# Two picks a step instead of sixteen in one go: moving the scatters of the first attention's groups

## The chip, the cores and the metric

The kernel runs on one core of a Trainium2 chip. The metric is the device time of one execution in microseconds (us). The kernel before took 1837.02 us (median of three runs, 1831.98 to 1838.97).

## The reference

Two decoder layers on 16 sequences of 128 tokens and 256 channels. What the change touches lies in the first layer:

```python
x = x + attention(layernorm(x))           # 16 heads of 128
x = x + wkv(layernorm(x), ctx)            # per channel: a recurrence over the 128 tokens
h = layernorm(x)
probs = softmax(h @ router_w.T)           # 16 experts
top_vals, top_idx = top_k(probs, 4)       # four picks for every token
x = x + sum of the picked experts of h, weighted by top_vals, + a shared expert
```

Attention, a further cross attention and a ternary feed-forward of the second layer follow and are not touched.

## The kernel before, in words

The work is laid out by hand, engine by engine. There are four groups (g = 0 to 3) of four sequences. The first attention walks over 16 projections p (a group times a set of four heads), and each has four steps, one per sequence: NSTEP = 64 steps, n = 4p + b. The groups come one after the other: group 0 in steps 0 to 15, group 1 in 16 to 31, and so on.

In step n every engine does its part of three sequences at once: TensorE (PE) computes the scores of n (line 763), turns the probabilities of n - 2 (771), fills in three of the twelve parts of the next projection's queries, keys and values (595 to 597), multiplies the output of n - 3 (790) and the values of n - 2 (780). VectorE (DVE) takes a value part out of PSUM (1657), masks and reduces the scores (1663, 1666), normalises (1671, 1673) and adds the output to the residual (1680). ScalarE (ACT) takes the exponentials (2342) and copies the turned probabilities and the values out of PSUM (2350, 2355). PE may not start the output of the next sequence before DVE has added the last one (line 1680).

Beside these steps runs the next layer's work for the group whose attention is done. It is written as generators, and `side.step` advances each engine's own list by five moments per step. In step 20 (36, 52) the list of group 0 (1, 2) is added: `wkv_group` (39 moments, the recurrence in two halves of 128 channels), `routing` (25, the layer norm of the routed rows, the logits, the top four) and `dispatch` (9, where in the table of picked rows each pick goes). GpSimd (POOL) has three kinds of work there:

- `split_wqkv` (2702, 2704): it splits a third of the next projection's weights in two parts of lower precision. The load of a third is issued by SyncE (SP, `fetch_third`, 2925), which waits until the raw buffer is free, that is for an earlier split. In the third step of a projection (b = 2; 34, 38, 42 ...), once PE has done an output that SP waits for, SP issues the output weights and then zeros and weights in turn: six transfers of 512 KB.
- `wkv_helps` (2710, 2711): two products of the recurrence. They wait for ACT's exponentials, and DVE waits for them.
- `scatter(g, b)` (2723 to 2731): four indirect DMAs for sequence b of the group, one for each pick. Each writes 128 rows of 1 KB to the table `picked_inputs` in DRAM, at the rows that DVE put in `slots` (1478). They read the group's normalised rows in `tiles_xn`, one of two buffers.

The next user of that buffer is `normalised` of the next group's routing (1251 to 1262), on DVE: it waits until all sixteen scatters of the group have landed. The last reader of the table is the expert stage, after the attention.

## Time and profile before

| | us |
|---|---|
| median of three runs | 1837.02 |
| all three | 1831.98, 1838.97, 1837.02 |
| profiled execution: its own time | 1832.67 |
| its span in the trace | 1830.9 |
| PE busy | 1622.8 (89%) |
| DVE busy | 1132.0 (62%) |
| ACT busy | 971.9 (53%) |
| POOL busy | 537.7 (29%) |

The span goes from the first instruction to the end of the last. The busy shares are averages over stages with different limits; the stage of the change lies between about 35 and 620 us. The starts of PE's scores (line 763) mark the steps of the attention. A row of the order of time (timeline) gives start, duration, engine, line, operation and tiles, and in brackets how long the engine had been idle before, and what ended that; "remote" there is a semaphore whose update came from no instruction that the trace shows ending at that time, "issue" is idle time for which the profile shows no wait.

### The profile page before, as it was taken

How to read it: one execution, taken by the hardware profiler on the slowest of the kernel's cores; microseconds unless marked ns; L12 is line 12 of the kernel's file. 1: busy time of each engine (PE TensorE's matmuls, PEld its weight loads, DVE VectorE, ACT ScalarE, POOL GpSimd, SP SyncE). 2: the span in 40 equal slices, each digit the busy share in tenths (PEclk: the TensorE clock that was granted, in tenths of full speed). 3: DMA queues.
4: the chain of work that ended last, by engine and by line, in shares of the span. 5: the costliest groups of instructions: out<-in, count | busy, mean ns of one | idle time of the engine just before them, and what ended most of it. 6: DMA issues, size and time to landing. Idle time of an engine off the chain costs nothing. (4 is left out here: it accounts for less than half of the span.)

```text
span 1830.9 us, 25838 instructions
## 1 busy us (share of the span) xinstructions
PE 1622.8 (89%) x8598; PEld 1303.0 (71%) x8598; DVE 1132.0 (62%) x2496; ACT 971.9 (53%) x2789; POOL 537.7 (29%) x447
## 2 busy tenths in 40 slices
PE   6999989889988768899999859999889999999866
PEld 5888877778777656667777647777667887888634
DVE  4654685577577676354443464643447778767878
ACT  4645545445454553223323545677747666676756
POOL 2242332733442271311002365445022122211000
PEclk9999999999999989999999957988789999999989
DMA  7153333422543162143433311000030111000001
GB/s 271 47 178 110 124 139 126 170 98 98 185 149 108 43 166 64 58 127 108 130 106 125 116 46 30 27 4 24 1 135 20 42 40 33 13 1 1 1 1 47
DMA packets 87512, 151.50 MB, mean 83 GB/s; under 512 B 9941, under 2 KB 45397, under 8 KB 87381
## 3 DMA queue, kind: packets, MB, share of 16 engines
q1 hardware_dynamic: 81236, 133.07, 22.2%
q0 software_dynamic: 6144, 16.79, 2.9%
q8 instruction: 70, 1.15, 0.3%
q14 instruction: 62, 0.50, 0.1%
HBM read 90.84 MB, written 58.98 MB: 82 GB/s over the span
## 5 line engine op out<-in xcount | busy, mean ns | idle before, releaser
L790 PE MATMUL bank<-self_attention 128*128 128x256 f32 x512 | 127.7, 394 | 26.4 <-DVE residual L1680 18.1
L2598 ACT ACTIVATE cross_attention_heads<-cross_attention_heads,small 128x128 f32<-128x128 f32 x256 | 99.6, 390 | 89.2 <-DVE small L2033 89.2
L2342 ACT ACTIVATE self_attention<-self_attention,small 128x128 f32<-128x128 f32 x256 | 100.0, 392 | 83.7 <-DVE small L1666 83.2
L1126 PE MATMUL bank<-cross_attention,cross_attention_heads 128*128 128x256 f32 x512 | 125.0, 387 | 15.3 <-DVE residual L2047 10.0
L790 PEld LDWEIGHTS bank<-self_attention 128*128 128x128 f32 x512 | 98.2, 195 | 46.5 <-DVE residual L1680 24.4
L595 PE MATMUL bank<-x_channel_major,qkv_weights_split 128*128 128x512 f32 x256 | 117.8, 460 | 7.3 <-DVE qkv_weights_split L1698 2.9
L1126 PEld LDWEIGHTS bank<-cross_attention,cross_attention_heads 128*128 128x128 f32 x512 | 95.9, 192 | 38.8 <-DVE residual L2047 18.9
L2510 ACT ACTIVATE narrow_late<-bank,small 128x128 f32<-128x128 f32 x256 | 91.0, 376 | 58.2 <-DVE small L1904 57.5
L2702 POOL CAST qkv_weights_split<-self_attention 128x1024 fp32r<-128x1024 f32 x45 | 50.6, 1125 | 223.0 <-DMA self_attention<-in_wqkv 198.5
L2704 POOL TENSOR_TENSOR qkv_weights_split<-self_attention,qkv_weights_split 128x1024 fp32r<-128x1024 f32 x45 | 109.5, 2433 | 3.6
L888 PE MATMUL bank<-experts,tiles 128*128 x316 | 108.0, 465 | 0.4 <-DVE tiles L1782 0.4
L596 PE MATMUL bank<-x_channel_major,qkv_weights_split 128*128 128x512 f32 x256 | 102.9, 402 | 0.0
L597 PE MATMUL bank<-x_channel_major,qkv_weights_split 128*128 128x512 f32 x256 | 102.5, 400 | 0.0
L1657 DVE TENSOR_TENSOR self_attention<-bank,self_attention 128x512 f32<-128x512 f32 x64 | 43.5, 684 | 88.6 <-PE bank L597 62.3
L2902 POOL TENSOR_TENSOR cross_attention_heads<-cross_attention 128x512 f32<-128x512 f32 x32 | 35.2, 1100 | 201.6 <-DVE cross_attention L2009 201.5
L1904 DVE TENSOR_REDUCE small<-bank 128x4 f32<-128x512 f32 x64 | 43.3, 682 | 69.4 <-PE bank L987 69.4
L1100 PEld LDWEIGHTS bank<-context_keys,cross_attention_heads 128*128 128x128 f32 x512 | 66.7, 192 | 27.0 <-issue 26.8
L2350 ACT COPY self_attention<-bank 128x512 f32<-128x512 f32 x64 | 37.5, 587 | 88.6 <-PE bank L771 79.2
L905 PE MATMUL bank<-experts_far,tiles 88*128 x316 | 81.2, 379 | 0.0
L1787 DVE TENSOR_TENSOR experts<-experts,bank 128x176 f32<-128x176 f32 x79 | 26.7, 338 | 86.6 <-ACT experts L2447 86.6
L1005 PEld LDWEIGHTS bank<-narrow_attention,narrow_late 128*128 128x128 f32 x512 | 71.5, 216 | 3.5 <-ACT narrow_late L2517 3.3
L2902 POOL TENSOR_TENSOR cross_attention_heads<-cross_attention_heads 128x512 f32<-128x512 f32 x32 | 35.2, 1099 | 132.1 <-DVE cross_attention_heads L2009 132.1
(398 smaller groups left out, 4725.1 us busy)
## 6 DMA issues: line engine op xcount, KB each, us to landing
picked_inputs<-self_attention SPq DMA_DIRECT2D x64, 512.0 KB
self_attention<-in_wqkv SPq DMA_DIRECT2D x48, 512.0 KB
experts_far<-picked_inputs SPq DMA_DIRECT2D x79, 128.0 KB, 2.1
picked_outputs<-tiles SPq DMA_DIRECT2D x79, 128.0 KB, 1.7
self_attention<-in_wo SPq DMA_DIRECT2D x16, 512.0 KB
experts<-in_moe SPq DMA_DIRECT2D x4, 1408.0 KB
self_attention<-in_bv SPq DMA_DIRECT2D x16, 256.0 KB, 5.1
context_values<-context_out SPq DMA_DIRECT2D x16, 256.0 KB
```

The lines of the kernel that those rows point to most:

```text
L595: T.matmul(out_ap, w_hi, x_hi, start=first, stop=False)
L596: T.matmul(out_ap, w_hi, x_lo, start=False, stop=False)
L597: return T.matmul(out_ap, w_lo, x_hi, start=False, stop=last)
L790: m = T.matmul(bank[7][:, 0:D], ZT_a[n % 2][:, h, :], wo_a[p % 2][:, h, :], start=h == 0, stop=h == HG - 1)
L888: m = T.matmul(bank[2 + n % 2][:, 0:2 * EI].rearrange("p (m c) -> p m c", m=2), t_xT[n % 2][:, k, :], wup[:, :, k, bass.ds(at, EI)], start ...
L905: m = T.matmul(bank[6 + n % 2][:, 0:D], t_hT[n % 2][0:HALF, i, :], wdown[0:HALF, i * D:(E - 1) * 2 * D + (i + 1) * D][:, bass.ds(at, D)], ...
L1005: m = T.matmul(bank[6][:, hh * DS:(hh + 1) * DS], n_PT[n % 2][:, h, :], n_v[bb % 8][:, hh * DS:(hh + 1) * DS], start=True, stop=True)
L1126: m = T.matmul(bank[7][:, 0:D], ZT_x[n % 2][:, h, :], x_wo[hg % 2][:, h, :], start=h == 0, stop=h == HG - 1)
L2342: m = S.activation(P_a[u][:, h, :], P_a[u][:, h, :], ACT.Exp, bias=negmax_a[u][:, h:h + 1], accum_out=sums_a[u][:, h:h + 1])
L2510: m = S.activation(n_P[v][:, h, :], s4_in[:, h, :], ACT.Exp, bias=n_negmax[v][:, h:h + 1], accum_out=n_sums[bb % 2][:, q4 * 4 + h:q4 * 4 + ...
L2598: m = S.activation(P_x[u][:, h, :], P_x[u][:, h, :], ACT.Exp, bias=negmax_x[u][:, h:h + 1], accum_out=sums_x[u][:, h:h + 1])
L2704: G.tensor_tensor(wqkv[m][1], third(t), wqkv[m][0].bitcast(F32), ALU.subtract).then_inc(w_split, 1)
```

## The change

Groups 0 and 1 no longer scatter in `dispatch`. A second list, `slow`, is stepped twice in each step, each time in front of a `side.step`, and each time issues one pick (one indirect DMA). The list of group 0 is added in step 35, that of group 1 in step 51, so that each group's sixteen picks are spread over eight steps: 35 to 42 and 51 to 58. Groups 2 and 3 scatter as before, four in a row in `last_group` (group 3: sixteen in a row). The numbers of moments stay as they were, and nothing else is changed.

```diff
-            def scatter(g, b):
-                i = NORM["routing", g]
+            def scatter_pick(g, b, k):
+                i, c = NORM["routing", g], (g * GB + b) * TOPK + k
                 pool.wait_ge(slots_set, g + 1)
                 pool.wait_ge(*all_zeroed(g))
                 pool.wait_ge(ln_norm, GB * i + GB)
+                G.indirect_dma_start(picked_x, bass.IndirectOffsetOnAxis(slots[:, c:c + 1], 0), tiles_xn[i % 2][:, b, :],
+                                     None).then_inc(scattered, 16)
+
+            def scatter(g, b):
                 for k in range(TOPK):
-                    c = (g * GB + b) * TOPK + k
-                    G.indirect_dma_start(picked_x, bass.IndirectOffsetOnAxis(slots[:, c:c + 1], 0), tiles_xn[i % 2][:, b, :],
-                                         None).then_inc(scattered, 16)
+                    scatter_pick(g, b, k)
+
+            def slow_scatter(g):
+                for b in range(GB):
+                    for k in range(TOPK):
+                        scatter_pick(g, b, k)
+                        yield
 
             def dispatch(g):
-                yield from pause(5)
-                for b in range(GB):
-                    if g < NG - 2:
-                        scatter(g, b)
-                    yield
+                yield from pause(5 + GB)
...
+            slow = Side()
             for n in range(NSTEP + 3):
                 if n % 16 == 4 and 16 < n < NSTEP:
                     side.add(wkv_group(n // 16 - 1), routing(n // 16 - 1), dispatch(n // 16 - 1))
+                if n % 16 == 3 and n > 2 * 16:
+                    slow.add(slow_scatter(n // 16 - 2))
                 if n >= NSTEP - 1:
                     split_weights(n - NSTEP + 1)
+                slow.step()
                 side.step(2)
                 p, b = divmod(n, GB)
                 if b == 0 and 1 <= p < NHG * NG - 1:
                     split_wqkv(p + 1, 2)
                 elif b >= 2 and p + 2 < NHG * NG:
                     split_wqkv(p + 2, b - 2)
+                slow.step()
                 side.step(3)
...
             side.finish()
+            slow.finish()
```

On the other engines the order of the instructions is the same. On POOL, at the end of group 0's routing (steps 33 to 38), the kernel before has its picks in two runs, of twelve and of four, around the first split of the next projection:

```order
L2704 TENSOR_TENSOR qkv_weights_split<-self_attention,qkv_weights_split 128x1024
L2730 DMA picked_inputs<-normalised_tiles,dispatch 33024x256 x12
L2702 CAST qkv_weights_split<-self_attention 128x1024
L2704 TENSOR_TENSOR qkv_weights_split<-self_attention,qkv_weights_split 128x1024
L2730 DMA picked_inputs<-normalised_tiles,dispatch 33024x256 x4
L2702 CAST qkv_weights_split<-self_attention 128x1024
L2704 TENSOR_TENSOR qkv_weights_split<-self_attention,qkv_weights_split 128x1024
L2702 CAST qkv_weights_split<-self_attention 128x1024
L2704 TENSOR_TENSOR qkv_weights_split<-self_attention,qkv_weights_split 128x1024
```

With the change, the same stretch (the last split ahead of the picks is left out, and the recurrence's first products end it) reads:

```order
L2728 DMA picked_inputs<-normalised_tiles,dispatch 33024x256
L2702 CAST qkv_weights_split<-self_attention 128x1024
L2704 TENSOR_TENSOR qkv_weights_split<-self_attention,qkv_weights_split 128x1024
L2728 DMA picked_inputs<-normalised_tiles,dispatch 33024x256 x2
L2702 CAST qkv_weights_split<-self_attention 128x1024
L2704 TENSOR_TENSOR qkv_weights_split<-self_attention,qkv_weights_split 128x1024
L2728 DMA picked_inputs<-normalised_tiles,dispatch 33024x256 x4
L2710 TENSOR_TENSOR wkv<-wkv 128x4x128
L2711 TENSOR_TENSOR wkv<-wkv 128x512
```

The picks stand behind the first split, one, two and four of them, and the four are followed by the products of the recurrence's first half.

Between the two halves of group 1's recurrence (steps 38 to 42), the kernel before has splits alone on POOL:

```order
L2702 CAST qkv_weights_split<-self_attention 128x1024
L2704 TENSOR_TENSOR qkv_weights_split<-self_attention,qkv_weights_split 128x1024
L2702 CAST qkv_weights_split<-self_attention 128x1024
L2704 TENSOR_TENSOR qkv_weights_split<-self_attention,qkv_weights_split 128x1024
L2702 CAST qkv_weights_split<-self_attention 128x1024
L2704 TENSOR_TENSOR qkv_weights_split<-self_attention,qkv_weights_split 128x1024
L2710 TENSOR_TENSOR wkv<-wkv 128x4x128
L2711 TENSOR_TENSOR wkv<-wkv 128x512
```

and the changed one has the other nine picks, the last of them just behind the first split of step 42:

```order
L2702 CAST qkv_weights_split<-self_attention 128x1024
L2704 TENSOR_TENSOR qkv_weights_split<-self_attention,qkv_weights_split 128x1024
L2728 DMA picked_inputs<-normalised_tiles,dispatch 33024x256 x2
L2702 CAST qkv_weights_split<-self_attention 128x1024
L2704 TENSOR_TENSOR qkv_weights_split<-self_attention,qkv_weights_split 128x1024
L2728 DMA picked_inputs<-normalised_tiles,dispatch 33024x256 x2
L2702 CAST qkv_weights_split<-self_attention 128x1024
L2704 TENSOR_TENSOR qkv_weights_split<-self_attention,qkv_weights_split 128x1024
L2728 DMA picked_inputs<-normalised_tiles,dispatch 33024x256 x3
L2710 TENSOR_TENSOR wkv<-wkv 128x4x128
L2711 TENSOR_TENSOR wkv<-wkv 128x512
L2728 DMA picked_inputs<-normalised_tiles,dispatch 33024x256
```

In all there are 1, 2, 4, 2, 2, 3, 1 and 1 picks between other work, where there were 12 and 4. Group 1's picks stand in the same way, but its last two directly follow each other, since the splits have ended by then.

## Rows read from the trace of the kernel before

**Rows 1.** Windows: two steps of group 0's stretch and one of group 1's
```profile
core 0: us, PE busy (x) PEld busy (x) DVE busy (x) ACT busy (x) POOL busy (x), PEclk, DMA share, GB/s
335.13:343.27 8.14, 8.14 (x48) 7.13 (x46) 1.38 (x2) 4.66 (x13) 6.08 (x7) 1.00 0.48 141
343.27:357.70 14.43, 10.03 (x47) 8.22 (x46) 5.18 (x8) 3.41 (x11) 12.29 (x11) 0.88 0.97 350
499.05:514.99 15.94, 10.58 (x48) 8.60 (x46) 5.16 (x8) 3.40 (x11) 13.47 (x13) 0.79 0.92 324
```
**Rows 2.** Timeline of PE: the two waits
```profile
343.04 0.40 PE L597 MATMUL bank<-qkv_weights_split,x_channel_major 128*128 128x512 f32 x1
...
344.16 0.60 PE L771 MATMUL bank<-identity,self_attention 128*128 128x128 f32 x4
...
345.76 0.40 PE L597 MATMUL bank<-qkv_weights_split,x_channel_major 128*128 128x512 f32 x1
350.56 2.96 PE L790 MATMUL bank<-self_attention 128*128 128x256 f32 x8 [4.40 <-DVE residual L1680]
...
507.29 3.78 PE L790 MATMUL bank<-self_attention 128*128 128x256 f32 x8 [5.36 <-DVE residual L1680]
```
**Rows 3.** Timeline of DVE: the same two stretches
```profile
336.94 0.69 DVE L1666 TENSOR_REDUCE small<-self_attention 128x4 f32<-128x512 f32 x1
349.48 0.69 DVE L1657 TENSOR_TENSOR self_attention<-bank,self_attention 128x512 f32<-128x512 f32 x1 [11.85 <-issue]
...
506.22 0.69 DVE L1657 TENSOR_TENSOR self_attention<-bank,self_attention 128x512 f32<-128x512 f32 x1 [12.81 <-remote]
```
**Rows 4.** Timeline of ACT, first stretch
```profile
350.32 0.59 ACT L2350 COPY self_attention<-bank 128x512 f32<-128x512 f32 x1 [4.46 <-remote]
```
**Rows 5.** Timeline of POOL, first stretch
```profile
332.98 1.18 POOL L2730 DMA_INDIRECT picked_inputs<-normalised_tiles,dispatch  x1 [6.33 <-DVE dispatch L1478]
...
348.09 1.05 POOL L2702 CAST qkv_weights_split<-self_attention 128x1024 fp32r<-128x1024 f32 x1
...
355.84 0.97 POOL L2730 DMA_INDIRECT picked_inputs<-normalised_tiles,dispatch  x1 [0.30 <-issue]
```
**Rows 6.** Windows: SP's six transfers without picks; single picks later in the program
```profile
382.00:392.00 10.00, 10.00 (x57) 8.71 (x56) 9.24 (x11) 4.34 (x16) 3.77 (x4) 1.00 0.84 300
1103.00:1137.00 34.00, 31.57 (x171) 25.61 (x169) 16.26 (x30) 19.04 (x71) 17.75 (x18) 0.79 0.08 24
```
**Rows 7.** Timeline, group 3's sixteen picks in a row: PE, then DVE
```profile
751.98 0.39 PE L597 MATMUL bank<-experts_split 128*128 128x512 f32 x1
755.23 0.69 DVE L1738 TENSOR_TENSOR experts<-experts,bank 128x512 f32<-128x512 f32 x1 [5.61 <-remote]
```
**Rows 8.** Timeline, group 2's second run of four picks: POOL, then ACT
```profile
658.31 1.19 POOL L2730 DMA_INDIRECT picked_inputs<-normalised_tiles,dispatch  x1 [0.30 <-issue]
664.89 0.62 ACT L2419 CAST experts_split<-experts 128x512 fp32r<-128x512 f32 x1 [5.04 <-DVE experts L1738]
```
**Rows 9.** Timeline of SP and POOL: a weight load, products and a split
```profile
340.74 0.62 SPq L2925 DMA_DIRECT2D self_attention<-in_wqkv  x1
...
416.80 2.18 POOL L2710 TENSOR_TENSOR wkv<-wkv 128x512 f32<-128x512 f32 x1 [13.79 <-ACT wkv L2241]
...
432.12 2.71 POOL L2704 TENSOR_TENSOR qkv_weights_split<-self_attention,qkv_weights_split 128x1024 fp32r<-128x1024 f32 x1
```
**Rows 10.** Waits between 100 and 620 us, one row
```profile
PE bank L595 <- POOL qkv_weights_split L2704: 2.0, 2, 1.3
```
**Rows 11.** Timeline of DVE: the norm that waits for the scatters
```profile
441.86 1.85 DVE L1261 TENSOR_SCALAR normalised_tiles<-residual,small 128x256 f32<-128x256 f32 x4
```
**Rows 12.** Page, part 6: the loads of the value bias, us to landing
```profile
self_attention<-in_bv SPq DMA_DIRECT2D x16, 256.0 KB, 5.1
```
**Rows 13.** Timeline of DVE: beside POOL's first pick, and beside POOL's products
```profile
333.18 0.69 DVE L1673 TENSOR_TENSOR self_attention<-self_attention,small 128x512 f32<-128x512 f32 x1
...
381.06 1.49 DVE L1344 TENSOR_TENSOR wkv<-wkv 128x512 f32<-128x512 f32 x1
```

## The prediction

> **What bounds the kernel now.** I read the page first: PE is busy for 89% of the span, so a stretch in which PE waits is what can be won. Then the windows of the attention, one per step. An undisturbed step takes 8.14 us, all of it PE [rows 1] (its first row). Two steps, 35 and 51, take 14.43 and 15.94 us [rows 1]. They are the longest of the attention, and both lie behind the long run of twelve picks. The recurrence has slow steps too (10 to 13 us), but those are there in group 0's recurrence as well, where no pick is issued.
>
> Then the order of time in step 35. PE issues its last part at 345.76 and stands for 4.40 us until DVE has added an output; in step 51 for 5.36 us [rows 2]. DVE in its turn had nothing to compute: from 337.6 to 349.48 it was idle, 11.85 us, and 12.81 us in the second case [rows 3]. It waited to take a value part out of PSUM (line 1657) that PE had finished at 343.4 [rows 2]. ACT, which does not depend on DVE there, is late in the same way: its copy of line 2350 starts at 350.32, after an idle time that ends "remote" [rows 4], although PE's transposes for it had ended at 344.8 [rows 2]. So it is no single engine or operand that is late. Updates of semaphores reach the waiting engines some 6 us after the work is done.
>
> What runs at the time is POOL: picks from 332.98 to 348.09, one every 1.27 us, then a split, then four more until 356.8 [rows 5]. SP's six 512 KB transfers start in the same stretch, and the DMA share is 0.97 in step 35 [rows 1]. Two comparisons tell the two apart. The same six transfers run elsewhere without picks, at a share of 0.84, and PE has no idle time there [rows 6] (the first row). And group 3's sixteen picks run without any transfer of SP's: there too a part that PE finished at 752.4 is only taken by DVE at 755.23, "remote" [rows 7]. I conclude that a long run of picks holds up the updates, and that SP's transfers make it start earlier.
>
> **The change, part by part.**
> *The long run goes.* Twelve picks and four become runs of 1, 2, 4, 2, 2, 3, 1 and 1, with splits of some 3.8 us or waits between them. If nothing is held up, steps 35 and 51 take 8.14 us: 14.43 - 8.14 = 6.29 and 15.94 - 8.14 = 7.80, together **14.1 us**. 9.8 of them are PE's idle time [rows 2]; the other 4.3 are its slower pace behind it: the granted clock was 0.88 and 0.79 of full in these steps, and the eight matmuls of line 790 took 2.96 and 3.78 us [rows 1, 2]. Group 2's and group 3's runs stay, with their waits.
>
> *The sixteen picks of a group are added to steps 35 to 42* (51 to 58). A pick takes POOL 0.96 to 1.35 us with 0.30 between two. What stands behind each run:
> - Step 34's split now stands ahead of all picks. Its load was issued at 340.74 [rows 9] and the split began at 348.09, right behind the twelfth pick [rows 5]; now it begins then or earlier, and ends by 351.6. PE, no longer held, wants these weights 1.2 us into step 36: at 343.3 + 8.1 + 1.2 = 352.6. It is free, with a us to spare. All of the attention has two waits of PE for a split, the longer 1.3 us [rows 10]; I count none here.
> - The four in a row (36 to 38) end near 367, and the products behind them wait for ACT, until 379.83 in this trace. Free.
> - The pairs push the splits of steps 39 and 40 back by 2.6 us each, to about 400 and 406; PE uses them a step or two later. Free.
> - The three in a row then end at 410 and the second products start at 416.80 [rows 9]. Free, with 6.8 us to spare.
> - The sixteenth pick comes behind the split that ended at 434.83 [rows 9], beside a weight load, a zero and a bias of SP's. DVE's norm of the next routing starts at 441.86 [rows 11], 7.0 us later. The nearest landing in the profile, of 256 KB under the same load, takes 5.1 us [rows 12]. I take nothing, and 0 to 1 us for the range. It is the one wait that the change tightens: everything of DVE's stands behind it, PE's next output included.
>
> *Does a pick slow DVE?* Beside the first pick DVE's normalisation took 0.69 us, its usual time; beside POOL's products one of the same size (line 1344) took 1.49 [rows 13]. So the products cost DVE something and a pick does not. The Trainium skill (SBUF — State Buffer, section on the two separate sides) says that GpSimd writes a DMA's descriptors through the port pair that it shares with VectorE, and gives 3100 ns for a transfer of 620 ns beside a VectorE copy. By its factor of five, an estimate, a pick would be 4.85 us beside such work; the rows do not show that, and it is a rival below.
>
> *Are updates held up behind the short runs?* The bounds: single and paired picks between 1103 and 1137 us go with no "remote" wait at all, PE busy for 31.57 of 34 us [rows 6] (the second row): zero. Four picks beside a large load of SP's (the last ends at 659.5) are followed by a cast of ACT's that had stood for 5.04 us [rows 8]: at most 5.0 per run of three or more, 15 for a group if the four pairs behave as one more. I take 1.0 us per group, near the lower end, because SP is nearly silent when the four and the three are issued. Both groups: +2.0.
>
> **Sum:** -14.1 + 2.0 = -12.1 us. Against the profiled execution's own 1832.67 that is 1820.6; the median of the runs lies 4.35 us higher, and against it the forecast is 1837.0 - 12.1 = **1825 us**.
>
> **The rivals.**
> - *The hold-up only moves.* The 4, the 2 + 2 and the 3 of a group hold the updates for some 2 us each, in steps where the chain DVE - ACT - POOL - DVE has no slack: 3 x 2 x 2 groups = 12 back of 14.1, and 1835. For it: group 2's four [rows 8]. Against it: the single picks [rows 6]. 21%.
> - *The transfers were the cause.* Then steps 35 and 51 stay as they are and the time is 1837. Against it: [rows 6, 7]. 9%.
> - *The picks wait for DVE.* They move beside the recurrence, where DVE is busiest. If each were held for as long as two products take (2.18 us each [rows 9]), there are 1.27 + 4.36 = 5.6 us from pick to pick, the three end at 406.2 + 16.9 = 423.1, the second products start 6.3 us late in both groups, and the time is 1825 + 12.6 = 1838. It decides from 3.5 us a pick. Against it: the picks beside DVE's work in this trace, none over 1.5 us. 3%. The page on SBUF would make it 406.2 + 3 x 5.15 = 421.7, so 1835.
> - *Slower: the updates are held up in the recurrence.* PE's slow steps 38 to 40 hang on several hand-overs in a row, so one hold-up is paid more than once. At 5.0 us for the four and for the three of both groups it is 20 us, and as much as 30 with the pairs, against 14.1 won: 1843 to 1853. It decides from 7.05 us per group. It needs SP's load as in [rows 8], which the four and the three do not have. 7%.
>
> **How the numbers follow.** A measurement tells 0.5% (9.2 us) from no change; faster by more than that is below 1827.8. The forecast has 60%. It stays below the line unless over 4.9 us come back. So faster 0.60; same 0.33 (the first three rivals); slower 0.07 (the fourth). The lowest time is all of 14.1 and nothing back, 1823, less the 4.35 us by which executions differ: 1818. The highest takes in the first rivals, 1837.
>
> **What would show it.** Right: steps 35 and 51 at about 8 us with no idle time of PE before line 790; no "remote" wait of DVE or ACT between 337 and 352; the steps of the recurrence as long as before. Wrong: a "remote" wait of 3 us or more behind the four or the three picks; DVE idle before the norm of line 1261 until a scatter lands; PE waiting for a split in step 36; the products starting later than ACT's exponentials. If steps 35 and 51 are still 14 us long, the cause is not the run of picks.

## The result and the profile after

| | before | after |
|---|---|---|
| median of six runs beside each other, us | 1834.50 (1829.11 to 1840.02) | 1818.03 (1810.71 to 1820.83) |
| ratio, 95% interval | | 0.9900 (0.9869 to 0.9931) |
| the same comparison once more (below) | 1829.73 | 1816.92, ratio 0.9933 (0.9909 to 0.9958) |
| profiled execution: its own time / its span | 1832.67 / 1830.9 | 1811.18 / 1809.4 |

By these ratios the change makes the kernel faster, by 18 us in the first comparison and by 12 us in the second (the medians lie 16.5 and 12.8 us apart). The two intervals share 0.9909 to 0.9931, which is 13 to 17 us. The forecast of 12 us lies inside the second and just outside the first.

The group of line 790 on the page, of the kernel before and then of the changed one (its last two numbers are PE's idle time before it, and what ended most of it):

```profile
L790 PE MATMUL bank<-self_attention 128*128 128x256 f32 x512 | 127.7, 394 | 26.4 <-DVE residual L1680 18.1
```

```profile
L790 PE MATMUL bank<-self_attention 128*128 128x256 f32 x512 | 122.2, 381 | 17.4 <-ACT self_attention L2355 9.1
```

PE stood for 26.4 us before line 790 in the kernel before, mostly for DVE's line 1680; now it is 17.4 us, mostly for ACT's copy (2355). Windows of the changed kernel: steps 35 and 51, and the five steps of the recurrence behind each of them:

```profile
core 0: us, PE busy (x) PEld busy (x) DVE busy (x) ACT busy (x) POOL busy (x), PEclk, DMA share, GB/s
340.89:349.02 8.13, 8.13 (x47) 7.14 (x46) 4.38 (x8) 2.82 (x10) 4.32 (x3) 1.00 0.85 312
490.09:498.22 8.13, 8.13 (x47) 7.14 (x46) 4.38 (x8) 2.82 (x10) 3.84 (x3) 1.00 0.88 304
349.02:400.50 51.48, 44.98 (x243) 38.31 (x242) 39.69 (x60) 25.39 (x68) 34.40 (x25) 0.97 0.42 143
498.22:550.07 51.85, 45.05 (x243) 38.48 (x242) 40.53 (x60) 25.39 (x68) 34.51 (x26) 0.97 0.43 143
```

Windows of the kernel before, the same five steps behind each run of picks:

```profile
357.70:408.97 51.27, 44.46 (x244) 38.12 (x243) 39.71 (x60) 25.29 (x68) 21.67 (x12) 0.97 0.27 93
514.99:566.63 51.64, 44.58 (x243) 38.34 (x242) 40.53 (x60) 25.29 (x68) 20.73 (x11) 0.97 0.26 88
```

Steps 35 and 51 take 8.13 us instead of 14.43 and 15.94 [rows 1], all of it PE, though the DMA share is as high as 0.85 and 0.88. The steps 36 to 40 take 51.48 us instead of 51.27, the steps 52 to 56 take 51.85 instead of 51.64. So in this pair of profiles the picks in the recurrence cost next to nothing. DVE and ACT of the changed kernel at the places of [rows 3] and [rows 4]:

```profile
341.09 0.69 DVE L1657 TENSOR_TENSOR self_attention<-bank,self_attention 128x512 f32<-128x512 f32 x1 [5.84 <-PE bank L597]
346.94 0.69 DVE L1657 TENSOR_TENSOR self_attention<-bank,self_attention 128x512 f32<-128x512 f32 x1 [2.10 <-PE bank L597]
349.22 0.69 DVE L1657 TENSOR_TENSOR self_attention<-bank,self_attention 128x512 f32<-128x512 f32 x1 [1.59 <-PE bank L597]
...
350.55 0.58 ACT L2350 COPY self_attention<-bank 128x512 f32<-128x512 f32 x1 [2.14 <-PE bank L771]
```

DVE takes its value parts (line 1657) as soon as PE has them: 5.84 us of idle time instead of 11.85, and no "remote" any more.

The spans of the two profiled executions differ by 21.5 us, and not all of that is the change. Read from the starts of line 763: 2.4 us of it lie ahead of step 35, 14.1 in steps 35 and 51, 1.5 in steps 41 to 50 and 57 to 63, 4.0 behind the attention; the recurrences give 0.4 back. Of the 7.9 us outside, only steps 41, 42, 57 and 58 hold anything that was changed, the last picks of each group. The rest are steps such as 22, which took 12.07 us before and 10.45 after, and takes 12.09 or 10.45 in other executions of this study.

### The profile page after: what moved, and what is told of

Its sections match the earlier page's. It is cut to its first block and busy times, and to the rows that moved or that the text cites. A ratio compares the mean times of both kernels' runs of the same rounds, so it can differ in the third digit from the quotient of the medians.

```text
span 1809.4 us, 25838 instructions
## 1 busy us (share of the span) xinstructions
PE 1610.7 (89%) x8598; PEld 1292.1 (71%) x8598; DVE 1128.6 (62%) x2496; ACT 972.1 (54%) x2789; POOL 540.4 (30%) x447
## 5 line engine op out<-in xcount | busy, mean ns | idle before, releaser
L790 PE MATMUL bank<-self_attention 128*128 128x256 f32 x512 | 122.2, 381 | 17.4 <-ACT self_attention L2355 9.1
L2728 POOL DMA_INDIRECT picked_inputs<-normalised_tiles,dispatch x64 | 68.2, 1065 | 17.8 <-issue 16.4
```

The lines of the kernel that those rows point to most:

```text
L790: m = T.matmul(bank[7][:, 0:D], ZT_a[n % 2][:, h, :], wo_a[p % 2][:, h, :], start=h == 0, stop=h == HG - 1)
```

## The experiments

Each kernel was timed beside the kernel before, on the same chip; the sets ran on different chips. Differences in us are worked out from the ratio, unless medians are named. The sums of steps are read from the one profiled execution of each kernel:

| kernel | ratio, 95% interval | step 35 | steps 36 to 40 | step 51 | steps 52 to 56 |
|---|---|---|---|---|---|
| before | 1 | 14.43 | 51.27 | 15.94 | 51.64 |
| the change | 0.9900 (0.9869 to 0.9931) | 8.13 | 51.48 | 8.13 | 51.85 |
| the change again (e8) | 0.9933 (0.9909 to 0.9958) | 8.13 | 52.80 | 8.13 | 51.96 |
| e1: none of the 32 picks | 0.9927 (0.9905 to 0.9949) | 8.13 | 52.61 | 8.13 | 53.15 |
| e2: group 0 only | 0.9970 (0.9954 to 0.9985) | 8.13 | 53.69 | 17.13 | 50.96 |
| e3: half of SP's load | 1.0010 (0.9991 to 1.0028) | 11.17 | 53.16 | 15.64 | 53.61 |
| e4: behind the split, nine in a row | 0.9910 (0.9885 to 0.9936) | 8.13 | 52.48 | 8.13 | 51.80 |
| e5: picks of 32 rows | 1.0032 (1.0009 to 1.0055) | 16.40 | 52.84 | 16.96 | 52.27 |
| e6: sixteen in steps 36 to 38 | 1.0034 (1.0011 to 1.0057) | 8.13 | 57.55 | 8.13 | 55.69 |
| e7: runs of 4, 8, 4 | 0.9959 (0.9941 to 0.9978) | 8.13 | 54.78 | 8.13 | 56.41 |
| e12: runs of 2, 4, 8, 2 | 0.9907 (0.9880 to 0.9933) | 8.13 | 53.18 | 8.13 | 53.19 |
| e13: twelve, SP's transfers later | 1.0050 (1.0021 to 1.0078) | 14.96 | 57.19 | 12.53 | 58.67 |
| e14: e6 with more load | 1.0056 (1.0028 to 1.0084) | 8.13 | 66.31 | 8.13 | 66.21 |
| e15: DVE kept busy | 1.0085 (1.0059 to 1.0111) | 14.02 | 60.95 | 15.57 | 59.15 |
| e16: a filler before every second pick | 0.9960 (0.9935 to 0.9985) | 8.13 | 55.86 | 8.13 | 55.79 |

### How much there was to win

**e1_no_picks.** Groups 0 and 1 are not scattered at all; the waits count accordingly.

```diff
-                if n % 16 == 3 and n > 2 * 16:
-                    slow.add(slow_scatter(n // 16 - 2))
```

> Leaves out the picks of groups 0 and 1 (their rows are not scattered), so that nothing of them can hold up anything: the most that any placing of these picks can win. Theory A (a long run of picks held up the updates; the changed kernel pays 1.8 us a group because its picks push a split beside DVE's norm): steps 35 and 51 take 8.1 us, steps 37 and 53 take 8.6 as before instead of 10.3 and 10.5, and the time is 3 to 5 us below the changed kernel, about 1814. Rival B (the picks in the recurrence still hold up updates somewhere): more than 6 us below the changed kernel. Rival C (the steps 37 and 53 are longer for a reason that has nothing to do with the picks' place): they stay over 10 us and the time is that of the changed kernel.

1815.46 us, a ratio of 0.9927, which is 13.4 us. Steps 37 and 53 are back at 8.58 us, as theory A had it, but the time is not 3 to 5 us below the changed kernel: steps 39 and 40 (12.35 and 12.27) and 54 to 56 took up what was won. Its recurrences are even longer than the changed kernel's. So, as far as the intervals tell, the change gets all that moving these picks can bring, some 13 us, and its 1.8 us in step 37 are not on the path of the five steps as a whole. B and C fall too.

**e2_group0_only.**

```diff
-                if n % 16 == 3 and n > 2 * 16:
+                if n == 35:
```

> The change for group 0 alone; group 1's sixteen picks stay in runs of twelve and four. Theory A: step 35 takes 8.1 us, step 37 10.3; steps 51 and 53 as in the kernel before, 15.9 and 8.6. The gain is half, 6 to 8 us against the kernel before. If the hold-up hung on something else that the first group's burst sets up, step 51 would change too.

1825.06, 5.5 us below by the ratio (2.7 to 8.4). Step 35 is 8.13, step 51 17.13 with 6.09 us of idle time. The groups are two separate cases of the same thing.

**e8_change_again** is the changed kernel itself.

> The changed kernel once more, for the size of the gain on this chip beside the other runs of this set: 12 us below the kernel before by my sum; 14 to 16 if the first comparison was right that nothing is given back; the second profile also shows what of the difference between the two first profiles (21.5 us of span) repeats: steps 35 and 51 at 8.1, the steps 36 to 40 and 52 to 56 within 1 us of 51.5 and 51.9.

Its median is 12.8 us below the kernel before. Steps 35 and 51 repeat; 36 to 40 are 1.3 us longer than expected, 52 to 56 within 0.1. The profiled span is 1811.7 us, 19.2 below the kernel before's, of which 14.1 are again steps 35 and 51. The rest is made up otherwise than in the first profile: the two recurrences are 1.9 us longer than before instead of 0.4, and the part behind the attention is 7.6 us shorter instead of 4.0. So differences of a few us outside steps 35 and 51 are not to be read as the change's.

### What holds the updates up

**e3_small_zeros** and **e13_transfers_later** leave the run of twelve where it was and take from SP's load beside it.

```diff
+                if i in (37, 38, 39, 54, 55, 56):
+                    D_(picked_x[at:at + 1, :], zero_a[0:1, 0:D]).then_inc(zeroed[g % 2], 16)
+                    return
```
```diff
+                if i in (37, 54):
+                    sp.wait_ge(scattered, 16 * (12 if i == 37 else GB * TOPK + 12))
```

(The first edit is e3's, the second e13's.)

> The kernel before with its picks as they were, but the three 512 KB zero transfers of step 34 and the three of step 50 are one row each (these rows are not zeroed), so that half of SP's load beside the long run of picks is gone. Theory A (the run of picks alone): steps 35 and 51 stay at 12 to 16 us and the time is within 4 us of the kernel before. Rival D (the transfers were the cause, or both are needed): the steps fall to 8 to 10 us and 8 to 14 us are won. If the hold-up only starts later in the run, steps 35 and 51 take 10 to 12.

> The kernel before, but SP issues the zero and weight transfers of step 34 (50) only when the run of twelve picks has landed; only the transfer of line 2932 is left beside the run. The weights come late, so the steps are long whatever holds; what is read is DVE's first value part (line 1657) behind the run. If SP's transfers take part in the hold-up, DVE takes it within 0.2 us of PE's end and step 35 loses its idle time to a wait for the split in step 36 instead. If the run alone does it, DVE is idle for 11 to 13 us again and PE waits 4 to 6 us before line 790.

e3: the time is that of the kernel before. Step 35 was 3.3 us shorter, with 2.20 us of PE's idle time, but step 51 15.64 with 5.41. e13 shows it better, since only the transfer of line 2932 is left beside the run. Its timeline of DVE, then PE, group 0; then PE, group 1:

```profile
347.79 0.69 DVE L1657 TENSOR_TENSOR self_attention<-bank,self_attention 128x512 f32<-128x512 f32 x1 [11.90 <-remote]
...
348.87 3.78 PE L790 MATMUL bank<-self_attention 128*128 128x256 f32 x8 [4.45 <-DVE residual L1680]
...
509.60 3.20 PE L790 MATMUL bank<-self_attention 128*128 128x256 f32 x8 [2.49 <-issue]
```

In group 0 DVE stands for 11.90 us and PE for 4.45, as in [rows 3] and [rows 2]. In group 1 updates are late too (a copy of ACT's stands for 6.63 us, "remote"), but PE stands for only 2.49 us instead of 5.36, and step 51 takes 12.53 us instead of 15.94. So the six transfers are not needed for a hold-up. That they have no part in its size is not shown: in e3 and in e13 one of the two groups lost about half of PE's idle time, in each case another one. (e13's ratio of 1.005 goes with the late splits: steps 37, 52 and 56 take 14.1 to 14.3 us.)

**e5_small_picks.**

```diff
+                    r = slice(0, P if g >= NG - 2 else 32)
-...slots[:, c:c + 1], 0), tiles_xn[i % 2][:, b, :],
+...slots[r, c:c + 1], 0), tiles_xn[i % 2][r, b, :],
```

> The kernel before, its long runs in place, but each of the 32 picks of groups 0 and 1 takes 32 rows instead of 128 (the other 96 rows of a block are left out). Theory A1 (the hold-up grows with the descriptors that a run of picks has in flight): steps 35 and 51 fall to 8 to 9 us and 12 to 16 us are won. Theory A2 (the twelve instructions in a row hold up the updates, whatever they carry): the steps stay at 12 to 16 us and the time is that of the kernel before; unless a pick of 32 rows is much shorter than 1 us, then the run is shorter and the gain in between.

A2 holds. The timelines of POOL and PE, groups 0 and 1:

```profile
331.89 0.88 POOL L2731 DMA_INDIRECT picked_inputs<-normalised_tiles,dispatch  x1 [0.31 <-issue]
...
348.34 0.80 PE L595 MATMUL bank<-qkv_weights_split,x_channel_major 128*128 128x512 f32 x1 [3.98 <-ACT self_attention L2335]
...
509.62 0.79 PE L595 MATMUL bank<-qkv_weights_split,x_channel_major 128*128 128x512 f32 x1 [6.83 <-ACT self_attention L2335]
```

A pick of 32 rows is hardly shorter (0.87 us instead of 0.96), and PE stands for 3.98 and 6.83 us behind the run. The trace also has the times of the semaphore updates. In the first run those of the picks' own transfers arrive all along, from 332.6 to 344.3. Those of PE's lines 780, 597, 763 and 771, which PE had done between 338.7 and 344.4, arrive between 347.6 and 347.9, some 3 us after the last pick; the landings of SP's transfer and the last of the picks' own arrive there too, from 347.3 to 348.2. So PE's updates are held back while those of the earlier picks pass, and a quarter of the rows changes nothing.

**e15_vector_busy.** Eighteen small operations a step give DVE work beside the run; the function is called three times in each step.

```diff
+            def idle_work(n):
+                if n in (34, 35, 50, 51):
+                    for _ in range(6):
+                        V.tensor_tensor(product[:, 0:2], product[:, 2:4], product[:, 2:4], ALU.mult).then_inc(dve.own, dve.tick())
+                        dve.settle()
```

> The kernel before, with eighteen small DVE multiplications a step added in steps 34, 35, 50 and 51, where DVE was idle for 12 us beside the run of picks (they write scratch that nobody reads). Where no update was late, in steps 36 to 38, DVE was busy 7 to 9 us of each step. If it is DVE's work that lets the updates through, steps 35 and 51 fall from 14 to 16 us to 8 to 10. If DVE's idleness is only the consequence, they stay.

Steps 35 and 51 stay at 14.02 and 15.57. DVE does the eighteen operations from 334.1 to 339.9 and then stands for 5.80 us all the same, "remote" (6.95 in group 1): its idle time is a consequence. (The added work costs some 8 us in each of steps 36 and 52; so the total says nothing.)

**e16_fillers.** The picks stay where they were, but ahead of every second one POOL does a small multiplication and waits for its end (`settle`).

```diff
+                    if g < NG - 2 and k % 2 == 0:
+                        G.tensor_tensor(product[:, 0:2], product[:, 2:4], product[:, 2:4], ALU.mult).then_inc(pool.own, pool.tick())
+                        pool.settle()
```

> The kernel before with one small multiplication of POOL's ahead of every second pick of groups 0 and 1 (scratch that nobody reads): the run of twelve becomes six pairs less than 1 us apart, at the same place and under the same load. If a short break in the run is enough, steps 35 and 51 take 8 to 10 us and 10 to 14 us are won with the picks left where they were. If the picks' rate or place is what counts, they stay at 14 to 16.

Timelines of POOL, DVE and PE, then the windows of steps 35 and 51:

```profile
331.88 0.98 POOL L2733 DMA_INDIRECT picked_inputs<-normalised_tiles,dispatch  x1 [0.30 <-issue]
332.88 0.42 POOL L2730 TENSOR_TENSOR dispatch<-dispatch 128x128 f32<-128x128 f32 x1
333.57 1.01 POOL L2733 DMA_INDIRECT picked_inputs<-normalised_tiles,dispatch  x1 [0.28 <-POOL dispatch L2730]
...
339.46 0.69 DVE L1657 TENSOR_TENSOR self_attention<-bank,self_attention 128x512 f32<-128x512 f32 x1 [5.84 <-PE bank L597]
342.54 0.68 DVE L1657 TENSOR_TENSOR self_attention<-bank,self_attention 128x512 f32<-128x512 f32 x1
...
505.06 0.50 PE L595 MATMUL bank<-x_channel_major,qkv_weights_split 128*128 128x512 f32 x1 [3.12 <-POOL qkv_weights_split L2704]
```

```profile
core 0: us, PE busy (x) PEld busy (x) DVE busy (x) ACT busy (x) POOL busy (x), PEclk, DMA share, GB/s
339.26:347.40 8.14, 8.14 (x48) 7.14 (x47) 4.38 (x8) 2.82 (x10) 6.34 (x9) 1.00 1.03 390
492.32:500.44 8.12, 8.12 (x47) 7.13 (x46) 4.38 (x8) 2.82 (x10) 6.32 (x9) 1.00 1.00 371
```

This is the plainest result of the study. A filler of 0.42 us, 0.71 us from the end of one pair to the next pick in place of 0.30, and nothing is held up: DVE takes its parts at once, steps 35 and 51 are 8.13 us, and the updates flow under the full load of SP (DMA share 1.03 and 1.00). Whether the filler's work or the wait for its end is what helps was not told apart. It wins 7 us and not 14; the run is now longer than before by the fillers and the split behind it late: PE waits 3.12 us for line 2704 in step 52 (3.08 in step 36).

### How long a run may be

**e4_behind_split**, **e12_two_a_half**, **e7_four_a_half** and **e6_sixteen_later** change how the sixteen are spread: 2 + 7 = nine in a row behind step 36's split; two or four picks in each half step; all sixteen behind step 36's split. The lines added, those taken out left away:

```diff
e4:  +                slow.step(3 if n % 16 == 5 else 1)
     ...
     +                if n % 16 == 4 and n > 2 * 16:
     +                    slow.add(slow_scatter(n // 16 - 2))
     +                slow.step({4: 2, 5: 3}.get(n % 16, 1))
e12: +                slow.step(2)     (at both places)
e7:  +                slow.step(4)     (at both places)
e6:  +                if n % 16 == 4 and n > 2 * 16:
     +                    slow.add(slow_scatter(n // 16 - 2))
     +                    slow.finish()
```

> The changed kernel with the first picks of a group behind the split of step 36 (52) and nine in a row up to step 38 (54), instead of one and two ahead of the splits. Theory A, as far as the splits go: DVE's norm (four tensor_scalars, line 1261) is back from 4.9 to 1.4 us and steps 37 and 53 from 10.3 and 10.5 to 8.6: 3.5 us won against the changed kernel, about 1814. If nine picks in a row hold up the updates although SP is quiet, a wait ending remote appears in steps 37 to 38 and 2 to 5 us a group come back: 1817 to 1824.

> The change with two picks a half step: runs of 2, 4, 8 and 2 between the splits and products. Between the changed kernel (longest run four, 12 to 16 us won) and four a half step (4, 8, 4: 7 us won, PE idle for 5.1 and 5.5 us in steps 38 and 54). If the length of the longest run decides, it is like the latter, 7 to 9 us won. If only the run that begins beside SP's transfers costs, it is like the change.

> The change with four picks a half step instead of one: a group's sixteen come in steps 35 and 36 as runs of 4, 8 and 4 with the splits between, at the place and under the SP load of the old burst's end. Theory A with a threshold between nine and twelve: nothing is held up, time as the changed kernel (1815 to 1820). Theory A without a threshold (each pick past the fourth costs): updates 2 to 4 us late in the run of eight, 4 to 8 us given back, 1820 to 1826. If the place alone decides, steps 35 and 36 are as long together as before, 23 us, and all is given back.

> All sixteen picks of a group in one run, behind the split of step 36 (52), where SP is quiet until step 38. Theory A (run length decides): updates are late by 3 to 6 us from about the fifth pick, PE waits in steps 37 and 38, and 8 to 14 us of the change's gain are given back: 1823 to 1830. Rival D' (a long run costs only beside SP's transfers or only at that place): as the changed kernel, about 1816. The run of nine in the last set held up one update by 3.3 us and another by 7.4 and cost next to nothing, so I lean to a small cost, 2 to 8 us.

e4 and e12 are like the change, with nine and eight in a row and SP quiet, so the length of the longest run is not the rule that I had tested e12 for. What I had written of e4 before e6 ran, one update held by 3.3 us and another by 7.4, is borne out by no row: the one wait there that is longer than in e1 is 0.95 us of DVE's before line 1663 at 370.94, for 0.19. e7 and e6 are slower, in the main not for the reason I had expected. Timelines of e7 (POOL, DVE, and DVE in group 1), then of e6 (POOL, DVE, ACT, and ACT in group 1):

```profile
369.56 1.05 POOL L2702 CAST qkv_weights_split<-self_attention 128x1024 fp32r<-128x1024 f32 x1
370.70 2.33 POOL L2704 TENSOR_TENSOR qkv_weights_split<-self_attention,qkv_weights_split 128x1024 fp32r<-128x1024 f32 x1
...
370.83 2.75 DVE L1337 SCALAR_TENSOR_TENSOR wkv<-wkv,channel_vectors 128x512 f32<-128x512 f32 x1
...
523.82 0.69 DVE L1663 TENSOR_TENSOR self_attention<-bank,self_attention 128x512 f32<-128x512 f32 x1 [2.04 <-remote]
```

```profile
377.95 0.96 POOL L2728 DMA_INDIRECT picked_inputs<-normalised_tiles,dispatch  x1 [0.31 <-issue]
378.94 1.21 POOL L2710 TENSOR_TENSOR wkv<-wkv 128x512 f32<-128x512 f32 x1
...
373.59 0.69 DVE L1346 TENSOR_TENSOR wkv<-wkv 128x512 f32<-128x512 f32 x1
380.18 2.29 DVE L1350 TENSOR_TENSOR_SCAN wkv<-wkv 128x516 f32<-128x516 f32 x1 [5.90 <-POOL wkv L2710]
...
375.59 0.69 ACT L2335 ACTIVATE self_attention<-bank,channel_vectors 128x512 f32<-128x512 f32 x1 [0.94 <-PE bank L597]
...
535.99 0.59 ACT L2350 COPY self_attention<-bank 128x512 f32<-128x512 f32 x1 [3.83 <-remote]
```

In e6 group 0's sixteen picks run from 356.52 to 378.91 and no engine waits long for a late update (ACT's 0.94 us at 375.59 is its usual wait). Group 1's sixteen, from 512.38 to 534.57, do hold some back at their end: ACT's copy of line 2350 starts at 535.99, "remote", 2.4 us after PE's transposes for it had ended at 533.55. What costs most is POOL's order: the products of line 2710 stand behind the picks, DVE waits 5.90 us for them and PE 5.35 us for DVE (group 1: 7.15 and 5.10). In e7 a split pushed back to 369.56 lies beside DVE's line 1337, which takes 2.75 us instead of 0.74, and PE waits 5.11 us in step 38. In group 1 line 1337 takes 1.63 us, and behind the run of eight DVE also stands for 2.04 us, "remote", for scores that PE had finished at 521.28, 2.5 us before. So there my expectation of updates 2 to 4 us late was right for one group of two; how the 5.46 us that PE waits in step 54 divide between the two causes is open.

**e14_later_loaded** is e6 with six more transfers of SP's.

```diff
+                if p in (10, 14):
+                    sp.wait_ge(a_scores, 38 if p == 10 else 54)
+                    for i in range(6):
+                        to = picked_y[i * 512:(i + 1) * 512, :].rearrange("(p a r) d -> p a (r d)", p=P, a=2)
+                        D_(to, zero_a.unsqueeze(1).broadcast_to([P, 2, 512])).then_inc(iotas_set, 16)
...
```

> The run of sixteen behind step 36's split once more, with six extra 512 KB transfers of SP's beside it (zeros into rows that are written later). In the last set this run, with SP quiet, held nothing up that the trace shows. If SP's load is what was missing, updates come 3 to 6 us late in steps 37 and 38 and the time is 5 to 15 us over that kernel's. If not, steps 37 and 38 stay at 8.6 and 10.4 and the time is within 4 us of it.

Steps 37 and 53 stay at 8.6, but steps 38 and 54 take 24.3 and 24.4. Timelines of DVE, ACT and PE:

```profile
369.45 0.42 DVE L1680 TENSOR_TENSOR residual<-bank,residual 128x256 f32<-128x256 f32 x1 [3.08 <-remote]
378.84 0.69 DVE L1663 TENSOR_TENSOR self_attention<-bank,self_attention 128x512 f32<-128x512 f32 x1 [8.10 <-remote]
...
374.41 0.69 ACT L2335 ACTIVATE self_attention<-bank,channel_vectors 128x512 f32<-128x512 f32 x1 [10.69 <-remote]
...
375.15 0.79 PE L595 MATMUL bank<-x_channel_major,qkv_weights_split 128*128 128x512 f32 x1 [5.38 <-ACT self_attention L2335]
```

The hold-up is back, 10.69 us of ACT's and 8.10 of DVE's, both "remote". So load makes a large hold-up of a run that without it held little (e6), and taking most of the load away from the other run does not remove it (e13). **Open:** why twelve picks under one transfer hold the update of PE's line 771 by 5.6 and 6.4 us (e13, groups 0 and 1) and sixteen in steps 36 to 38 hold it by 0.9 and 2.4 us (e6). In e6 single picks there take 1.86 and 1.70 us instead of 0.96; they start at 363.09 and 371.90, just behind the starts of DVE's scans of lines 1326 and 1341 (362.95 and 371.60). The pauses between the picks stay 0.30 us, so that these long picks act as the break of e16 does is a guess; it was not tried.

### The collision that I had not seen

In the changed kernel the pair of picks at 353.46 pushes step 36's split beside DVE's norm. Timelines of POOL and DVE of the changed kernel, then DVE of e4, whose picks come behind the split:

```profile
354.76 0.97 POOL L2728 DMA_INDIRECT picked_inputs<-normalised_tiles,dispatch  x1 [0.30 <-issue]
355.74 1.05 POOL L2702 CAST qkv_weights_split<-self_attention 128x1024 fp32r<-128x1024 f32 x1
356.87 2.36 POOL L2704 TENSOR_TENSOR qkv_weights_split<-self_attention,qkv_weights_split 128x1024 fp32r<-128x1024 f32 x1
...
355.14 4.90 DVE L1261 TENSOR_SCALAR normalised_tiles<-residual,small 128x256 f32<-128x256 f32 x4
```

```profile
358.64 1.39 DVE L1261 TENSOR_SCALAR normalised_tiles<-residual,small 128x256 f32<-128x256 f32 x4
```

The four operations take 4.90 us beside the split and 1.39 without it; step 37 is 10.34 us and 8.58. The Trainium skill (SBUF — State Buffer, section on who interferes with whom) says that VectorE in a two-port mode, which a tensor_scalar can enter, and a GpSimd operation take turns on a shared port pair, each for a whole instruction. The trace agrees for the four tensor_scalars: 3.5 us longer beside the split. Line 1337 in e7 is no tensor_scalar; that it too is longer beside a split (2.75 us for 0.74) is told by its row alone. No row of this study shows the same beside a pick.

### The same remedy elsewhere

**e9_paced_gathers**, **e10_paced_last**, **e11_paced_both**: the changed kernel, with the run of twenty gathers behind the expert stage cut into fours, with group 3's sixteen picks cut into pairs, and with both.

```diff
             for bb in range(7):
+                pool.wait_ge(c_proj, (0, 8, 13, 18, 23, 27, 30)[bb])
                 gather(bb)
```
```diff
-                for b in range(GB):
-                    scatter(NG - 1, b)
+                for j in range(GB * TOPK):
+                    if j % 2 == 0:
+                        pool.wait_ge(e_h_hi, NUNIT - 8 + j // 2)
+                    scatter_pick(NG - 1, j // TOPK, j % TOPK)
```

> The changed kernel with the run of twenty gathers at 972 to 998 us cut into fours, each waiting until PE has done five more of the context's projections (1.37 us each), so that some 1.8 us lie between two fours. If the run of picks holds up the updates there too, PE's idle times of 2.20 and 6.59 us before line 595 go: 6 to 9 us below the changed kernel, 1.0 to 1.3% below the kernel before. If a pause of 1.8 us is too short to let the updates through, or what follows waits for the last gathers instead (line 1756), the time is that of the changed kernel.

> The changed kernel with group 3's sixteen picks in pairs, each pair waiting for the next expert unit (4.2 us each). Theory A: PE's idle time of 6.97 us before line 852 at 741.5 falls to under 2 and 4 to 6 us are won against the changed kernel. The rows are read only after 765 us, when all eight pairs are through, so a loss needs the pairs to be over 10 us late. Rival: the idle time there is the end of a unit as in the three groups before (8.14, 2.90 us before the same line), and stays.

> Both of these: if the two gains stand by themselves they add, 10 to 15 us below the changed kernel and 1.4 to 1.8% below the kernel before. A gain below that of the better one alone would mean that one of the waits only moved.

| kernel | median, us | ratio, 95% interval |
|---|---|---|
| before, same chip | 1829.90 | 1 |
| e9 | 1806.29 | 0.9857 (0.9827 to 0.9886) |
| e10 | 1808.09 | 0.9871 (0.9840 to 0.9902) |
| e11 | 1798.47 | 0.9828 (0.9801 to 0.9856) |

PE's waits in the changed kernel, behind group 3's picks and among the gathers:

```profile
741.54 1.97 PE L852 MATMUL bank<-identity,experts 128*128 128x128 f32 x8 [6.97 <-ACT experts L2426]
...
990.75 0.50 PE L595 MATMUL bank<-context_weights_split,x_channel_major 128*128 128x512 f32 x1 [2.20 <-DVE context_keys L1853]
999.12 0.80 PE L595 MATMUL bank<-context_weights_split,x_channel_major 128*128 128x512 f32 x1 [6.59 <-issue]
```

and in e11, of the three only the first is left, behind a pair of picks:

```profile
742.41 1.14 PE L852 MATMUL bank<-identity,experts 128*128 128x128 f32 x8 [1.25 <-ACT experts L2426]
...
737.97 1.28 POOL L2728 DMA_INDIRECT picked_inputs<-normalised_tiles,dispatch  x1 [1.62 <-ACT experts_split L2419]
739.56 0.96 POOL L2728 DMA_INDIRECT picked_inputs<-normalised_tiles,dispatch  x1 [0.30 <-issue]
```

15.8 us of PE's waiting become 1.25. Where a run was left uncut its waits stay: 6.95 us before line 852 in e9, 3.18 and 7.62 before line 595 in e10. The gains add (differences of medians): e9 and e10 are 23.6 and 21.8 us below the kernel before, each with the change's own gain in it, and e11 31.4, so 14.0 are left for the change alone, between its two measurements. e11 is the fastest kernel of the study, 31 us below the kernel before.

## Why the prediction was right, and where it was not

The cause and the term of 14.1 us held. The step that failed is the term of +2.0 us for updates held up behind the short runs: the runs show nothing there, and without it the forecast is 2 us lower.

**The cause: right.** "A long run of picks holds up the updates." e2, e5, e13 and e16 show it from four sides: take the run from one group and only that group's step is cured; neither fewer rows nor fewer transfers remove it; a short break does. By what mechanism a run of picks delays the updates of PE is not shown. That "SP's transfers make it start earlier" was the weaker half. They can bring it about (e14) but were not needed here (e13); whether they make it larger is open.

**The 14.1 us: right, to 0.1 us** in steps 35 and 51 (8.13 each). Clock and idle time came back together, as summed.

**The +2.0 us for the short runs: wrong.** This is the term that was mis-sized. It was taken from the row of ACT behind group 2's four picks [rows 8], which names DVE as the releaser, and that was no late update. The row of DVE, of the kernel before:

```profile
664.20 0.66 DVE L1738 TENSOR_TENSOR experts<-experts,bank 128x512 f32<-128x512 f32 x1
```

It ends at 664.86, and ACT's cast starts at 664.89. In the changed kernel's two profiles no wait of the attention ends "remote". The recurrences took +0.2 us each in the first profile and +1.5 and +0.3 in the second, but e1, with no pick at all, has +1.3 and +1.5 and is no faster, so these are not the picks'. The term measured nothing that can be told from zero. The sum without it is -14.1, a ratio of 0.9923, inside both intervals.

**"It is free, with a us to spare": right for the split it was said of, but one question was not asked.** Step 34's split ended at 347.95 and PE began with its weights at 350.27, 2.3 us later. But the split of step 36, which two picks now precede, came beside DVE's norm, which took 3.5 us longer (4.90 for 1.39). I had asked who waits for a moved split, not who works beside it. That the time did not suffer is luck as far as the prediction goes. The 1.76 and 1.90 us that it cost in steps 37 and 53 came back within the same recurrence, as e1 and e4 show, so it is not in the time.

**Picks beside DVE: right.** They take 0.96 to 1.51 us in the first profile and 1.90 at most in the second; none was held for long. The wait that the change tightens, DVE's norm for the last pick of a group, did not show: that pick starts at 425.70 and the norm at 433.25, with no idle time before it.

**The rivals.** "The hold-up only moves" falls with e1 and with the traces, in which nothing is held behind the moved picks. "The transfers were the cause" falls with e13. "The picks wait for DVE" and "held up in the recurrence" never show.

**The size against the median.** Forecast 1825, measured 1818.0, 7 us below. Of these, 2.5 are the base: I took 1837.0 from three executions, and the kernel before had a median of 1834.5 in the comparison. 2.0 are the term above. The other 2.4 cannot be told from what executions differ by: single ones of the changed kernel span 10 us. The second comparison lies the other way, 1829.7 - 14.1 = 1815.6 against 1816.9 measured. The measured 1818.0 is also at the very edge of the range: its lowest time, given as 1818, is 1818.6 when it is not cut to a whole number. It was drawn too narrow on that side, since it allowed for how much executions differ but not for a base that was itself too high.

## What to carry to other kernels

Do not issue long unbroken runs of GpSimd's indirect DMAs beside work that is bound by semaphores: in this kernel PE's updates came 5 to 7 us late behind twelve picks, PE then stood for 2 to 7 us, and no engine looked guilty in the profile. Break the run with other work or with a wait after two to four of them; each further run that was cut gave 8 to 10 us (e11 against e10 and e9). When work is moved on POOL, look at what DVE does beside its new place, not only at who waits for it.

## What the hardware showed that I had not expected

- Picks that move a quarter of the rows hold up as much: PE waits 3.98 and 6.83 us with 32 rows (e5), 4.40 and 5.36 with 128.
- A break of some 0.7 us with a small operation in it, once per two picks, removes it under full DMA load (e16); pauses of 2.0 to 3.5 us between fours of gathers do so too (e9).
- DVE's four tensor_scalars took 1.39 us alone and 4.90 beside POOL's split; line 1337 0.74 and 2.75.
- Sixteen picks in a row can also pass and hold little (e6: PE's updates up to 1.3 us late in one group, up to 2.8 in the other), and the same sixteen with six transfers beside them leave ACT standing for 10.7 us (e14). What starts it is not settled.
